# The softmax gate of two MoE dispatches: subtraction on VectorE and one exponential, or one exponential per tile with a bias on ScalarE

## The chip, the cores and the metric

The kernel runs on 1 core of one Trainium2 chip. The metric is the device time of one execution in microseconds (us). The core has five engines with in-order queues of their own: TensorE (PE in the profile; its weight loads are PEld), VectorE (DVE), ScalarE (ACT), GpSimd (POOL) and SyncE (SP). They meet at semaphores.

## What is computed

The input is 256 images of 128 channels by 7 x 7 places, 12,544 tokens in all. Six layers follow each other: a windowed attention, a 1x1-convolution attention, an attention without weights, a mixture of experts (192 hidden), an attention over three strides, and a second mixture of experts (512 hidden). The change touches the gates of the two mixtures, of which the reference says:

```python
scores = jnp.einsum('bne,ex->bnx', x, Wg) + bg
topk_vals, topk_idx = jax.lax.top_k(scores, TOP_K)      # 2 of 8 experts
gates = jax.nn.softmax(topk_vals, axis=-1)
```

(the second mixture takes the softmax of all eight first and normalises the two picked, which is the same pair of numbers). With the two largest logits a >= b of a token, the kernel makes ex = exp(b - a), den = 1 + ex, first gate = 1/den, second gate = 1 - first gate.

## The kernel before

The program is a chain of phases: windows, convolution, token dispatch "d2", experts "moe2", combine, scales with dispatch "d3", experts "moe3", final. All tensors of a layer pass through DRAM or the SBUF tensor X between phases. The trace has the dispatch d2 at about 575 to 872 us and the scales with d3 at about 1245 to 1808 us.

**What a dispatch does.** The class Dispatch (from L1186) works on chunks of tiles of 128 tokens: d2 has 24 chunks of 4 tiles and one of 2, d3 has 32 chunks of 3 and one of 2, 98 tiles each. For a chunk, TensorE turns X into token rows (`turn`), VectorE takes mean and variance (`stats`), ScalarE makes the inverse deviation (`rstd`, L1360 and L1362) and writes the normed rows (`norm`, L1371). VectorE scales the logits (`scale`, L1446), and `choose` takes the eight largest of each tile (L1457), subtracts the first from the second for the whole chunk (`gap`, L1465) and looks up the indices (L1467, two records a tile). `count_up` marks the picked experts (`pick`, L1477) and counts them, TensorE sums the counts into ranks (L1331 to L1336), `place` turns them into row numbers (L1503, L1510), and `weigh` takes the reciprocal of den (L1496). On ScalarE `gate` makes ex (L1380) and den (L1384), `names` writes token number and index (L1392, L1394), `second` the other gate (L1401). GpSimd then sends each tile's rows to their places with two indirect DMAs (`scatter`, L1558): 196 in each dispatch. ScalarE and either VectorE (d2) or GpSimd (d3) also split the next layer's expert weights in two (L1351 on ScalarE, L1421 behind it).

**What sets the order.** Every engine runs a list of calls written out by hand, one step per group of 8 images (32 groups). In d2 the gate of a chunk runs one step after its `choose`, ScalarE's step being rstd, expo, rstd, gate, turned, norm, v_out, names, second, split_high, square. In d3 one chunk goes through each step, and a step has four parts, p = 0 to 3. On VectorE p = 1 ends with `choose`, p = 2 begins with the residual (L1917) and the next score block (L1869, L1873) and ends with `count_up` and `weigh`, p = 3 has `factors` (L1911) and `place`. On ScalarE p = 2 is q_out (L2083), expo (L2103), `gate`, turned (L2132), inverses (L2122, L2124), square (L2049) and k_out (L2092); p = 3 ends with logvar (L2067), `names`, `second` and, in every third step, the weight split L1351. GpSimd's step is: adding the positions (L2013), four products of probabilities (L2004), L1985, L1973 and L1974, L1995, two scatters in each of three parts, and in every third step the weight split L1421, which waits for L1351. TensorE's last transposition before each score block (L1775) waits until VectorE has emptied the score bank (L1873), and ScalarE's L2132 waits for that transposition.

The semaphores that matter: `gate` waits for gap_done and for the last den; `choose` waits for gap_done of the chunk before ahead of L1457, and for ex_done of the chunk before ahead of L1465.

Of the kernel before, what the change touches and what calls it, by code (L numbers as in the profile page):

```python
# [19 lines left out]
ALU = mybir.AluOpType  # L20
ACT = mybir.ActivationFunctionType
AX_X = mybir.AxisListType.X

C = 128
# [60 lines left out]
class PhaseSemaphores:  # L85


    def __init__(self, nc, prefix):
        self.nc, self.prefix, self.held = nc, prefix, []
# [1096 lines left out]
class Dispatch:  # L1186
# [7 lines left out]
    def __init__(self, nc, sh, sb, sem, kind, e, wsplit, rows_dram, chunks, xt, small, joint=False):  # L1194

        self.joint, self.nc = joint, nc
        self.chunks, self.wide = chunks, max(n for _, n in chunks)
        self.quads = [(c, t0 + o, min(4, n - o), o) for c, (t0, n) in enumerate(chunks) for o in range(0, n, 4)]
        self.last_quad = [max(q for q, quad in enumerate(self.quads) if quad[0] == c) for c in range(len(chunks))]
        self.sh, self.e, self.wsplit, self.rows_dram, self.xt, self.small = sh, e, wsplit, rows_dram, xt, small  # L1200
        self.wg, self.bg = (sh.wg2, sh.bg2) if kind == "d2" else (sh.wg3, sh.bg3)
        self.w_in, self.bias_in = (sh.inputs["L2_ffn_W"], sh.inputs["L2_ffn_b"]) if kind == "d2" else (sh.inputs["L3_ffn_W"], sh.inputs["L3_ffn_b"])
        self.wgc = sb("wgc", [C, C + EXPERTS])
        self.below, self.ones, self.base16 = sb("below", [C, C], BF16), sb("ones", [C, C], BF16), sb("base16", [C, EXPERTS], BF16)
        self.below_f, self.ones_f = sb("below_f", [C, C]), sb("ones_f", [C, C])
        self.base8, self.tokens = sb("base8", [C, EXPERTS]), sb("tokens", [C, TILES])
        self.upto8, self.steps, self.blocks = sb("upto8", [C, EXPERTS * EXPERTS]), sb("steps", [C, STEPS]), sb("blocks", [C, NBLK])
        self.pad = sb("pad", [C, BLOCK // C, ROW])
        self.raw = [sb(f"raw{i}", [C, e.half]) for i in range(2)]
        self.wh, self.wl = [sb(f"wh{i}", [C, e.half], F32R) for i in range(2)], [sb(f"wl{i}", [C, e.half]) for i in range(2)]  # L1210
        self.st, self.mv = sb("dst", [C, QUAD, 6]), [sb(f"mv{i}", [C, QUAD, 2]) for i in range(2)]
        self.rs = [sb(f"drs{i}", [C, self.wide]) for i in range(2)]
        self.row = [sb(f"row{i}", [C, self.wide, ROW]) for i in range(self.NR)]
        self.lg = sb("lg", [C, self.wide, EXPERTS])
        self.top, self.idx = sb("top", [C, self.wide, 8]), [sb(f"idx{i}", [C, self.wide, 8], U32) for i in range(2)]
        self.pick = [sb(f"pick{i}", [C, self.wide, 2, EXPERTS]) for i in range(2)]
        self.seen = [sb(f"seen{i}", [C, 1 + self.wide, EXPERTS], BF16) for i in range(2)]
        self.gap, self.ex, self.den = sb("gap", [C, self.wide]), sb("ex", [C, self.wide]), sb("den", [C, self.wide])
        self.at = sb("at", [C, self.wide, 2, EXPERTS])
        self.pos = [sb(f"pos{i}", [C, self.wide, 2], U32) for i in range(self.NR)]  # L1220
        self.total, self.offs = sb("total", [C, EXPERTS]), sb("offs", [C, EXPERTS], I32)
        self.over, self.full = sb("over", [C, EXPERTS, STEPS]), sb("full", [C, EXPERTS])
        self.ends8, self.ends = sb("ends8", [C, EXPERTS, EXPERTS]), sb("ends", [C, EXPERTS])
        self.past, self.gone = sb("past", [C, NBLK, EXPERTS]), sb("gone", [C, NBLK, EXPERTS])
        self.begun, self.where = sb("begun", [C, NBLK]), sb("where", [C, NBLK])

        self.loaded, self.ready, self.centred = sem("loaded"), sem("ready"), sem("centred_gate")
        self.raw_loaded = [sem(f"raw_loaded{i}") for i in range(2)]
        self.high, self.low = sem("w_high"), sem("w_low")
        self.w_stored = [sem(f"w_stored{i}") for i in range(2)]  # L1230
        self.b_stored = sem("b_stored")
        self.xt_mm, self.log_mm, self.stat, self.mean_var = sem("turned"), sem("logits"), sem("stats"), sem("mean_var")
        self.ln_done, self.rs_done, self.normed = sem("logvar_d"), sem("rstd_d"), sem("normed_d")
        self.scaled, self.top_done, self.idx_done = sem("scaled"), sem("top"), sem("index")
        self.pick_done, self.seen_done = sem("picked"), sem("seen")
        self.count_done, self.pos_mm = sem("counted"), sem("pos_mm")
        self.gap_done, self.ex_done, self.den_done, self.g0_done = sem("gap"), sem("exped_d"), sem("den"), sem("g0")
        self.col_done, self.named = sem("columns"), sem("named")
        self.at_done, self.pos_done = sem("at"), sem("positions")
        self.scattered = [sem(f"scattered{i}") for i in range(self.NR)]  # L1240
        self.total_mm, self.tab, self.padded = sem("total_mm"), sem("table"), sem("padded")
# [132 lines left out]
    def gate(self, act, c):  # L1374
        nt = self.chunks[c][1]
        act.wait_ge(self.loaded, 16 * 8)
        act.wait_ge(self.gap_done, c + 1)
        if c >= 1:
            act.wait_ge(self.den_done, c)
        act.activation(self.ex[:, 0:nt], self.gap[:, 0:nt], ACT.Exp).then_inc(self.ex_done, 1)  # L1380
        act.wait_ge(self.ex_done, c + 1)
        if c >= 1:
            act.wait_ge(self.g0_done, c)
        act.activation(self.den[:, 0:nt], self.ex[:, 0:nt], ACT.Identity, bias=self.ones_f[:, 0:1]).then_inc(self.den_done, 1)  # L1384
# [65 lines left out]
    def choose(self, dve, c):  # L1450
        nt = self.chunks[c][1]
        lg, top, idx = self.lg, self.top, self.idx[c % 2]
        dve.wait_ge(self.scaled, c + 1)
        if c >= 1:
            dve.wait_ge(self.gap_done, c)
        for i in range(nt):
            last = dve.max(top[:, i, :], lg[:, i, :])  # L1457
        last.then_inc(self.top_done, 1)
        dve.wait_ge(self.top_done, c + 1)
        if c >= 1:  # L1460
            dve.wait_ge(self.ex_done, c)
        if c >= 2:
            dve.wait_ge(self.named, 2 * c - 2)
            dve.wait_ge(self.pick_done, c - 1)
        dve.tensor_tensor(self.gap[:, 0:nt], top[:, 0:nt, 1], top[:, 0:nt, 0], ALU.subtract).then_inc(self.gap_done, 1)  # L1465
        for i in range(nt):
            last = dve.max_index(idx[:, i, :], top[:, i, :], lg[:, i, :])  # L1467
        last.then_inc(self.idx_done, 1)
# [1458 lines left out]
```

## Time and profile before

| | us |
|---|---|
| three timed runs | 2283.72, 2289.64 (median), 2291.57 |
| profiled execution, whole | 2285.74 |
| profiled execution, span of the trace | 2284.1 |
| mean granted TensorE clock of the span | 0.891 of full |

The page shares the span as PE 78%, DVE 71%, ACT 61%, POOL 62% busy. Those are averages over eight phases with different limits, so for one phase only the rows of its own stretch count. The profiled execution's time is 1.6 us over its span and lies 3.9 us under the median of the timed runs.

### The profile page before, as it was taken

To read this page: it belongs to the slowest core of one execution; us is meant where nothing else is said; L and a number is where in the kernel's file an instruction comes from. 1 tells how busy PE (TensorE), PEld (TensorE's weight loads), DVE (VectorE), ACT (ScalarE), POOL (GpSimd) and SP (SyncE) were. 2 spreads that over 40 slices of the span, in tenths; PEclk is the share of its full clock that TensorE was granted. 3 is DMA by queue.
4 is the path that set the end of the run, shared out by engine and by line. 5 is a ranking of instruction groups with operands and counts; after the bars stand their busy time and mean duration, and the time that the engine had idled before them with its cause. 6 is when DMAs were issued, how large, how long until landed. Compare 5 with 4: busy or idle time off the path is not lost. (4 is left out here: it accounts for less than half of the span.)

```text
span 2284.1 us, 52612 instructions
## 1 busy us (share of the span) xinstructions
PE 1787.9 (78%) x16257; PEld 1236.1 (54%) x16257; DVE 1618.3 (71%) x4634; ACT 1404.3 (61%) x3208; POOL 1414.1 (62%) x1485
## 2 busy tenths in 40 slices
PE   7999997998777744777764777777786299999974
PEld 3555554776566643555543344444444177777763
DVE  5888887787677643666654588888786378888864
ACT  5777775564666523555540788888885267777750
POOL 3655554010177773777776378888888557767765
PEclk9999998999989857999985898998897599999995
DMA  6000000000221134666647012111110367777748
GB/s 116 17 0 0 0 0 2 1 0 18 74 83 55 55 89 124 185 180 179 174 122 249 9 60 68 55 56 55 60 36 30 98 222 232 227 231 234 226 131 338
DMA packets 169828, 233.57 MB, mean 102 GB/s; under 512 B 60032, under 2 KB 131957, under 8 KB 162190
## 3 DMA queue, kind: packets, MB, share of 16 engines
q1 hardware_dynamic: 142446, 172.32, 25.2%
q0 software_dynamic: 26880, 52.27, 6.8%
q10 hardware_dynamic: 288, 6.42, 0.7%
q8 instruction: 99, 1.62, 0.3%
q14 instruction: 115, 0.94, 0.1%
HBM read 155.37 MB, written 79.23 MB: 103 GB/s over the span
## 5 line engine op out<-in xcount | busy, mean ns | idle before, releaser
L2682 POOL DMA_INDIRECT expert_out<-moe_yr,moe_to x448 | 493.0, 1100 | 259.8 <-DVE moe_yr L2661 139.2
L1558 POOL DMA_INDIRECT expert_rows<-d_row,d_pos x392 | 380.8, 971 | 181.9 <-issue 164.8
L2597 ACT ACTIVATE moe_ah<-moe_hps,moe_w 128x512 f32<-128x512 f32 (+1 forms) x336 | 230.2, 685 | 204.3 <-PE moe_hps L2547 199.6
L2638 DVE TENSOR_TENSOR moe_hl<-moe_ah,moe_hh 128x512 fp32r<-128x512 f32 (+1 forms) x336 | 235.2, 700 | 95.6 <-ACT moe_hh L2602 89.3
L1775 PE MATMUL scales_ptps<-ident,scales_pr 113*128 113x113 f32 x512 | 104.2, 306 | 98.1 <-DVE scales_sc L1873 62.5
L550 POOL TENSOR_TENSOR window_pr<-window_pr,window_rc 113x392 f32<-113x392 f32 x128 | 108.9, 851 | 107.3 <-DVE window_rc L494 107.3
L2545 PE MATMUL moe_hps<-moe_xh,moe_w 128*128 128x512 f32 (+1 forms) x336 | 138.3, 412 | 35.5 <-DMA moe_w<-moe_split 31.4
L2533 PE MATMUL moe_xps<-ident,moe_xb 128*128 128x128 f32 x448 | 72.5, 286 | 102.6 <-DMA moe_xb<-expert_rows 102.6
L1775 PEld LDWEIGHTS scales_ptps<-ident,scales_pr 113*128 113x128 f32 x512 | 65.3, 157 | 152.3 <-DVE scales_sc L1873 68.7
L2557 PE MATMUL moe_yps<-moe_hh,moe_w 128*128 128x512 f32 (+1 forms) x336 | 144.3, 429 | 0.9 <-DVE moe_hl L2638 0.9
L538 POOL TENSOR_TENSOR window_sc<-window_sc,window_mx 113x392 f32<-113x392 f32 x128 | 107.8, 842 | 50.6 <-DVE window_mx L468 49.8
L2547 PE MATMUL moe_hps<-moe_xh,moe_w 128*128 128x512 f32 (+1 forms) x336 | 134.9, 401 | 0.0
L2546 PE MATMUL moe_hps<-moe_xl,moe_w 128*128 128x512 f32 (+1 forms) x336 | 134.5, 400 | 0.0
L2558 PE MATMUL moe_yps<-moe_hl,moe_w 128*128 128x512 f32 (+1 forms) x336 | 133.9, 398 | 0.0
L2559 PE MATMUL moe_yps<-moe_hh,moe_w 128*128 128x512 f32 (+1 forms) x336 | 133.3, 397 | 0.0
L2533 PEld LDWEIGHTS moe_xps<-ident,moe_xb 128*128 128x128 f32 x448 | 53.6, 144 | 134.2 <-DMA moe_xb<-expert_rows 125.3
L657 ACT ACTIVATE window_pt<-window_ptps 128x452 f32<-128x452 f32 x128 | 69.8, 545 | 90.9 <-PE window_ptps L334 90.8
L2004 POOL TENSOR_TENSOR scales_pr<-scales_pr,scales_fac 113x416 f32<-113x416 f32 x128 | 114.1, 903 | 2.7 <-DVE scales_fac L1911 1.3
L2627 DVE TENSOR_TENSOR moe_xl<-moe_xps,moe_xh 128x512 fp32r<-128x512 f32 x112 | 76.4, 682 | 54.6 <-ACT moe_xh L2590 54.6
L1071 POOL TENSOR_TENSOR conv_pr<-conv_pr,conv_rc 113x196 f32<-113x196 f32 x32 | 16.5, 516 | 154.4 <-DVE conv_rc L1037 154.4
L2602 ACT ACTIVATE moe_hh<-moe_ah 128x512 fp32r<-128x512 f32 (+1 forms) x168 | 106.2, 632 | 5.3
L2636 DVE CAST moe_hh<-moe_ah 128x512 fp32r<-128x512 f32 (+1 forms) x168 | 85.3, 508 | 27.1 <-ACT moe_ah L2597 27.1
(286 smaller groups left out, 5218.5 us busy)
## 6 DMA issues: line engine op xcount, KB each, us to landing
moe_w<-moe_split SPq DMA_DIRECT2D x56, 1026.5 KB
moe_xb<-expert_rows SPq DMA_DIRECT2D x112, 264.0 KB, 3.0
moe_w<-moe_split SPq DMA_DIRECT2D x56, 449.5 KB
c_yy<-expert_out SPq DMA_DIRECT2D x28, 448.0 KB, 7.1
final_yy<-expert_out SPq DMA_DIRECT2D x28, 448.0 KB, 7.7
expert_out<-moe_yr,moe_to POOLq DMA_INDIRECT x448
X<-in_x SPq DMA_DIRECT2D x32, 196.0 KB
expert_rows<-d_row,d_pos POOLq DMA_INDIRECT x392
```

What stands on the lines that cost most here:

```text
L1558: pool.indirect_dma_start(out=self.rows_dram, out_offset=bass.IndirectOffsetOnAxis(ap=self.pos[j][:, i, k:k + 1], axis=0), in_=self.row[j] ...
L1775: last = pe.transpose(ptps[:, hp * R:(hp + 1) * R], pr[at.r][p][:, 2 * hp:2 * hp + 2, :].rearrange("q h k -> q (h k)"), ident[0:R, 0:R])
L2533: last = pe.transpose(xps[:, t * C:(t + 1) * C], xb[b % NX][:, t, 0:C], ident[:, :])
L2545: pe.matmul(out, ww[:, W1H + k * P:W1H + (k + 1) * P], xh[j][:, :], start=True, stop=False)
L2546: pe.matmul(out, ww[:, W1H + k * P:W1H + (k + 1) * P], xl[j][:, :], start=False, stop=False)
L2547: pe.matmul(out, ww[:, W1L + k * P:W1L + (k + 1) * P], xh[j][:, :], start=False, stop=True).then_inc(h_mm, 1)
L2557: pe.matmul(out, ww[0:P, W2H + k * C:W2H + (k + 1) * C], high, start=(k == 0), stop=False)
L2558: pe.matmul(out, ww[0:P, W2H + k * C:W2H + (k + 1) * C], low, start=False, stop=False)
L2559: pe.matmul(out, ww[0:P, W2L + k * C:W2L + (k + 1) * C], high, start=False, stop=(k == K - 1)).then_inc(y_mm, 1)
L2597: act.activation(ah[n % NH][0:P, :], hps[n % 3][0:P, :], func, bias=bias(b, k)[0:P]).then_inc(h_done, 1)
L2638: dve.tensor_tensor(hl[n % NH][0:P, :], ah[n % NH][0:P, :], hh[n % NH][0:P, :].bitcast(F32), ALU.subtract).then_inc(hl_done, 1)
L2682: pool.indirect_dma_start(out=y_dram, out_offset=bass.IndirectOffsetOnAxis(ap=to[j][:, t:t + 1], axis=0), in_=yr[j][:, t, :], in_offset=No ...
```

## The change

The exponential of a chunk becomes one exponential for each of its tiles. Its input is the largest logit with scale -1, and its bias is the second largest, read from SBUF per partition. The subtraction, its tensor and its semaphore go. `gate` waits for top_done (the end of L1457) in place of gap_done; `choose` waits for ex_done of the chunk before ahead of L1457, where it waited for gap_done, and the later wait goes.

```diff
@@ Dispatch.gate
         act.wait_ge(self.loaded, 16 * 8)
-        act.wait_ge(self.gap_done, c + 1)
+        act.wait_ge(self.top_done, c + 1)
         if c >= 1:
             act.wait_ge(self.den_done, c)
-        act.activation(self.ex[:, 0:nt], self.gap[:, 0:nt], ACT.Exp).then_inc(self.ex_done, 1)
+        for i in range(nt):
+            last = act.activation(self.ex[:, i:i + 1], self.top[:, i, 0:1], ACT.Exp, scale=-1.0, bias=self.top[:, i, 1:2])
+        last.then_inc(self.ex_done, 1)
@@ Dispatch.choose
         if c >= 1:
-            dve.wait_ge(self.gap_done, c)
+            dve.wait_ge(self.ex_done, c)
         for i in range(nt):
             last = dve.max(top[:, i, :], lg[:, i, :])
         last.then_inc(self.top_done, 1)
         dve.wait_ge(self.top_done, c + 1)
-        if c >= 1:
-            dve.wait_ge(self.ex_done, c)
         if c >= 2:
             dve.wait_ge(self.named, 2 * c - 2)
             dve.wait_ge(self.pick_done, c - 1)
-        dve.tensor_tensor(self.gap[:, 0:nt], top[:, 0:nt, 1], top[:, 0:nt, 0], ALU.subtract).then_inc(self.gap_done, 1)
```

## Rows read from the trace of the kernel before

**Rows 1.** Busy time by stretch: length, PE, PEld, DVE, ACT, POOL, clock, DMA share, GB/s
```profile
575.00:872.00 297.00, 198.95 (x1623) 161.06 (x1621) 186.01 (x1009) 158.09 (x565) 188.73 (x196) 0.80 0.23 71
1335.00:1808.00 473.00, 345.27 (x4632) 213.84 (x4631) 372.76 (x1291) 360.33 (x915) 402.31 (x453) 0.86 0.17 55
```
**Rows 2.** GpSimd's groups, 620 to 868 us: busy, mean ns | idle before, releasers
```profile
L1558 POOL DMA_INDIRECT expert_rows<-d_row,d_pos x196 | 188.7, 963 | 121.3 <-issue 117.0 <-ACT d_row L1401 3.7 <-DVE d_pos L1510 0.3
```
**Rows 3.** GpSimd's waits, 1336 to 1808 us: total us, times, longest
```profile
POOL expert_rows L1558 <- issue: 47.8, 184, 1.4
POOL expert_rows L1558 <- ACT d_row L1401: 11.5, 6, 3.7
POOL d_wl L1421 <- ACT d_wh L1351: 6.7, 7, 1.9
POOL scales_wf L1995 <- ACT scales_rc L2124: 3.4, 3, 2.2
```
**Rows 4.** GpSimd's timeline in the steady steps of d3: start, length us
```profile
1513.61 0.99 POOL L1985 TENSOR_TENSOR scales_part<-scales_ef,scales_sm 113x384 f32<-113x384 f32 x1
...
1528.07 0.99 POOL L1985 TENSOR_TENSOR scales_part<-scales_ef,scales_sm 113x384 f32<-113x384 f32 x1
...
1531.52 0.90 POOL L2004 TENSOR_TENSOR scales_pr<-scales_pr,scales_fac 113x416 f32<-113x416 f32 x1
...
1533.01 0.86 POOL L1995 TENSOR_TENSOR scales_wf<-scales_ef,scales_rc 113x384 f32<-113x384 f32 x1
...
1554.44 2.38 POOL L1421 TENSOR_TENSOR d_wl<-d_raw,d_wh 128x1024 f32<-128x1024 f32 x1 [1.91 <-ACT d_wh L1351]
```
**Rows 5.** VectorE's groups by shape, 1300 to 1800 us: busy, mean ns | idle before
```profile
L1465 DVE TENSOR_TENSOR d_gap<-d_top 128x3 f32<-128x3 f32 x32 | 26.2, 819 | 1.1
```
**Rows 6.** VectorE's timeline: a step behind the weight split, then the next step
```profile
1512.39 2.25 DVE L1465 TENSOR_TENSOR d_gap<-d_top 128x3 f32<-128x3 f32 x1
1514.56 0.08 DVE L1467 MATCH_VALUE_LOAD d_idx<-d_top,d_lg 128x8 f32 x1
...
1528.60 0.49 DVE L1465 TENSOR_TENSOR d_gap<-d_top 128x3 f32<-128x3 f32 x1
1529.01 0.08 DVE L1467 MATCH_VALUE_LOAD d_idx<-d_top,d_lg 128x8 f32 x1
...
1532.03 0.47 DVE L1477 TENSOR_TENSOR d_pick<-iota,d_idx 128x48 f32<-128x48 f32 x1
```
**Rows 7.** ScalarE's timeline in the same steps
```profile
1522.78 0.29 ACT L1401 ACTIVATE d_row<-d_row,d_ones_f 128x3 f32<-128x3 f32 x1
1522.97 0.52 ACT L2074 ACTIVATE scales_rs<-scales_rs 128x392 f32<-128x392 f32 x1
...
1530.58 0.22 ACT L1380 ACTIVATE d_ex<-d_gap 128x3 f32<-128x3 f32 x1
1530.83 0.30 ACT L1384 ACTIVATE d_den<-d_ex,d_ones_f 128x3 f32<-128x3 f32 x1
1531.57 0.55 ACT L2132 ACTIVATE scales_pt<-scales_ptps 128x452 f32<-128x452 f32 x1 [0.44 <-PE scales_ptps L1775]
...
1532.31 0.28 ACT L2124 ACTIVATE scales_rc<-scales_rc 113x96 f32<-113x96 f32 x1
```
**Rows 8.** TensorE's timeline; L1708 in two steps
```profile
1535.58 0.93 PE L1708 MATMUL scales_vps<-scales_sq,mean_w 128*128 128x392 f32 x2
...
1545.67 0.32 PE L1775 MATMUL scales_ptps<-ident,scales_pr 113*128 113x113 f32 x1 [1.84 <-DVE scales_sc L1873]
...
1550.74 1.68 PE L1708 MATMUL scales_vps<-scales_sq,mean_w 128*128 128x392 f32 x2
```
**Rows 9.** L1465's busy time on VectorE in a stretch, then clock, DMA share, GB/s
```profile
1548.00:1556.00 8.00, 0.00 (x0) 0.63 0.06 19
```
**Rows 10.** Timeline at the first chunk of d2
```profile
608.58 0.17 DVE L1465 TENSOR_TENSOR d_gap<-d_top 128x4 f32<-128x4 f32 x1
608.66 0.08 DVE L1467 MATCH_VALUE_LOAD d_idx<-d_top,d_lg 128x8 f32 x1
...
614.61 0.19 ACT L1380 ACTIVATE d_ex<-d_gap 128x4 f32<-128x4 f32 x1
...
617.51 0.32 ACT L1401 ACTIVATE d_row<-d_row,d_ones_f 128x4 f32<-128x4 f32 x1
...
618.86 1.14 POOL L1558 DMA_INDIRECT expert_rows<-d_row,d_pos  x1 [61.79 <-issue]
```

More of the change, by code:

```diff
@@ L1217, in __init__ @@
         self.seen = [sb(f"seen{i}", [C, 1 + self.wide, EXPERTS], BF16) for i in range(2)]
-        self.gap, self.ex, self.den = sb("gap", [C, self.wide]), sb("ex", [C, self.wide]), sb("den", [C, self.wide])
+        self.ex, self.den = sb("ex", [C, self.wide]), sb("den", [C, self.wide])
         self.at = sb("at", [C, self.wide, 2, EXPERTS])
@@ L1236, in __init__ @@
         self.count_done, self.pos_mm = sem("counted"), sem("pos_mm")
-        self.gap_done, self.ex_done, self.den_done, self.g0_done = sem("gap"), sem("exped_d"), sem("den"), sem("g0")
+        self.ex_done, self.den_done, self.g0_done = sem("exped_d"), sem("den"), sem("g0")
         self.col_done, self.named = sem("columns"), sem("named")
```

## Prediction, made before the changed kernel ran

> **What bounds the kernel now.** Only the two dispatches are touched, so I read their stretches and not the page's averages. First the busy time by stretch. In d2 no engine is busy throughout: GpSimd's 188.73 of 297 us is the scatters alone. In 1335 to 1808 us, where the scales phase sorts, GpSimd leads with 402 of 473 us, before DVE with 373 and ACT with 360 [rows 1]. Then what ends the idle time of that engine. In d2 its 196 scatters take 0.963 us each and are followed by about 0.3 us of issue; 188.7 + 117.0 us of issue (61.8 of which is the idle stretch before the first one) is 244, the whole time from the first scatter to the last. It waited for ScalarE in no way that one sees: 3.7 us in the same 0.3 us pieces [rows 2]. So d2 ends when GpSimd has issued its list, and the only thing that can move it is the start of the list.
>
> In d3 GpSimd's busy time and its 47.8 us of issue make 450 of 473 us. What is left is nearly all ScalarE's doing: 11.5 us in 6 waits for L1401, 6.7 us in 7 for the weight split L1351, 3.4 us in 3 for L2124, 21.6 us in 16 waits [rows 3]. Between them GpSimd is packed; a step without a weight split lasts 14.45 us on it (L1985 at 1513.61 and 1528.07 lie one step apart [rows 4]). **So time in d3 can only be won or lost at those 16 waits, or by a step that becomes longer than GpSimd's own.**
>
> **The row that surprises.** The subtraction of 128x3 numbers takes 819 ns on average in d3, 26.2 us for 32 [rows 5], where the same work with 4 columns takes 0.17 us in d2 [rows 10]. The timeline tells why. In one step it lasts from 1512.39 to 1514.64, and GpSimd's L1985 ends at 1514.60; in the next it lasts from 1528.60 to 1529.09, and L1985 ends at 1529.06 [rows 4, 6]. It ends 0.03 to 0.04 us behind a GpSimd product both times: it waits for GpSimd. The Trainium skill has the reason, SBUF — State Buffer, "Who interferes with whom": a VectorE instruction with two SBUF inputs and a GpSimd instruction that reads SBUF take one shared port in turn, each for its whole length. By that rule, the trace agrees.
>
> **The change part by part.** *VectorE, removed.* In d2 start to start the subtraction costs 608.66 - 608.58 = 0.08 us [rows 10]. In d3 it is 1529.01 - 1528.60 = 0.41 us in an ordinary step, and 1514.56 - 1512.39 = 2.17 us in the step behind a weight split, where GpSimd is late [rows 6].
> *Who gets it.* What follows on VectorE is the index search, with no stall in these rows, the residual and the score block, whose L1873 frees TensorE's last transposition, for which TensorE waited 1.84 us [rows 8] and ScalarE's L2132 0.44 us [rows 7]. So up to here the 0.41 us is real. Then comes L1477, also a two-input instruction: it runs 1532.03 to 1532.50, ending 0.08 us behind GpSimd's L2004 of 1531.52 to 1532.42. Begun 0.41 us earlier it begins at 1531.62, still inside L2004, and ends when it ends now [rows 4, 6]. So the part of the step behind L1477 gets nothing from an ordinary step, and up to 0.41 us where L1477 slips in ahead of L2004.
> *ScalarE, added.* 196 exponentials replace 58, all with a bias read from SBUF. No row shows an exponential with such a bias on one column. The nearest is L1401, 3 columns with bias and scale: 0.29 us long, but the next instruction starts 0.19 us behind it [rows 7]. The bounds per further start are 0.10 (the 0.29 us less 0.19 of overlap, a start that costs only its remainder) and 0.29 us (no overlap at all). I take 0.19, being the measured spacing of that form. The last one is 0.29 long where the old one was 0.19 to 0.22. With 3 tiles: 2 x 0.19 + 0.10 = +0.48 us; with 4 tiles 3 x 0.19 + 0.10 = +0.67 us. Bounds with 3 tiles 0.3 to 0.7 us.
> By the Trainium skill, ScalarE: Activation LUTs, "Rules for kernel authors", the budget is about 0.3 us for each activation with a bias pointer; taken as serial work, an estimate from it is 3 x 0.3 - 0.22 = +0.68 us a step, and d3 would then be the slower rival below.
> *What hides it in d3.* The gate ended at 1531.13 and L2132 began at 1531.57, behind a wait of 0.44 us that ends on VectorE's path [rows 7]. VectorE's path comes 0.41 us earlier, ScalarE's 0.48 us later: L2132 starts at 1531.61, +0.04 us. L2124 ends at 1532.59 + 0.04, GpSimd wants it at 1533.01 [rows 4]: 0.38 us to spare. If this cover were gone, each step would cost 0.48 us, 15.4 us for 32.
> *The 13 waits for L1401 and L1351.* These stand behind TensorE: in the step of the weight split GpSimd waited 1.91 us for L1351 [rows 4], the granted clock was 0.63 in that stretch [rows 9], which is a time partly at the lower level, and L1708, which ScalarE needs, took 1.68 in place of 0.93 us [rows 8]. TensorE began this run at 1545.67, released by L1873 [rows 8], which comes 0.41 us earlier without the subtraction. So each wait shrinks by between 0 (L1477 holds the later score block where it is) and 0.41 us. I take 0.3, nearer the upper end, since L1873 lies ahead of L1477: 13 x 0.3 = **-3.9 us**. The bounds are 0 and -5.3. The three waits for L2124 lie in the tail, behind 1727 us, where the subtraction no longer stalls; I take 0 for them, at most 3 x 0.48 = +1.4.
> *Steps behind a weight split* give VectorE 2.17 us, but GpSimd is packed there; 0 us, unless the lead survives to the next wait (a rival).
> *d2.* ScalarE runs without a gap from L1380 at 614.61 to L1401 at 617.51, and the first scatter follows that [rows 10]: +0.67 - 0.08 = **+0.6 us** at the start of a packed list. Bounds 0.2 and 1.0. The other 24 gates are hidden by the list.
> *Waits moved.* ex_done of the chunk before, now ahead of L1457: in d2 `weigh`, earlier in VectorE's step, has already waited for den, which comes behind ex; in d3 the gate is a step old. 0 us. Behind `weigh`'s wait for den in d3 the gate has over 1 us to spare.
> *Sum:* -3.9 + 0.6 = -3.3 us. Against the profiled execution, 2285.74 - 3.3 = 2282.4; the median of the runs lies 3.9 above it, so 2286.3.
>
> **The rivals.** *1, the lead is kept (faster).* The 2.17 us and the 0.41 us carry VectorE and ScalarE ahead through L1477 and on to the weight split; TensorE idles less and keeps its upper clock. GpSimd then never waits for L1351 or L1401. Of 6.7 + 11.5 us [rows 3] the first wait, 3.7 us, stays, as it is the filling of the pipeline: -14.5 + 0.6 = -13.9 us, 2275.7. For it: TensorE's wait of 1.84 us is VectorE's, and the 1.91 us depends on a clock that was down. Against it: TensorE's transpositions also need GpSimd's products, which come no sooner.
> *2, ScalarE becomes the one waited for (slower).* At the 16 places where GpSimd waits for ScalarE already, the gate stands in the same queue ahead of all three instructions. If ScalarE's waits for TensorE shrink away there, as VectorE's path gets shorter, each grows by 0.48 us: 16 x 0.48 = +7.7, with d2 +8.3 us, 2297.9. It decides as soon as a gate costs more than ScalarE waits behind it, 0.44 us in an ordinary step. At the upper bound of 0.7 us it would be 16 x 0.7 + 1.0 = +12. Against it: ScalarE's idle time in a step is several such waits, and L1351 is late through TensorE.
> *3, the stall only moves.* The change removes the subtraction but not the wait for GpSimd's port: L1477 or the next two-input instruction pays it, and nothing before it was late. d3 0, d2 +0.6: 2290.2, no change.
>
> **How the numbers follow.** About 0.3% (6.9 us) is what a measurement of this kernel tells from no change. The forecast has 0.45, its own range -6 to +3 and so "same"; rival 1 0.25, rival 2 0.15, rival 3 0.15. A tenth of rival 1 and of the others ends inside 0.3% too, as a partial effect. Faster 0.25, same 0.61, slower 0.14. The range for 8 in 10: below to rival 1's value less the spread of the runs, 2274; above, to the forecast's bounds and rival 3 with the runs' own spread of some 4 us, 2294, which leaves most of rival 2 out.
>
> **What would show it.** Right: L1380 with 196 records near 0.29 us, starting about 0.19 apart; GpSimd's list in d2 still without gaps and 0.6 us later; in d3 L2132's wait for TensorE close to 0, GpSimd's waits for L1351 shorter by about 0.3 each, and L1477 longer than its 0.47 us now. Wrong: those waits gone (rival 1) or each longer (rival 2), single activations spaced by 0.29 us, or a change of more than 7 us in the stretch 1335 to 1808 us; any change in the length of a phase other than the two dispatches would be no effect of this edit.

## The result, and the profile after

The changed kernel takes 2304.89 us in the median of four runs (2299.97 to 2308.60), the kernel before 2289.21 in four runs beside it (2283.72 to 2291.57). The ratio is 1.0074, 95% interval [1.0050, 1.0098]: it is slower, and 2304.89 lies above my range, which ended at 2294. I had forecast 2286.3 us and no change. The profiled execution took 2304.61 us with a span of 2302.8, 18.7 us above the span of before. In the experiments below, one run of one kernel (the marks reduced, 2721.34 us at a granted clock of 0.57) was in a slow state and is left out of its ratio.

In the changed kernel the lines behind the edit are renumbered: L1457 is L1459, L1467 is L1466, L1477 is L1476, L1482 is L1481, L1401 is L1403, L1558 is L1557, L1873 is L1872, L1775 is L1774, L1995 is L1994, L2004 is L2003, L2124 is L2123, L1421 is L1423 and L1351 keeps its number. L1465 is gone, and the exponentials are L1381.

First the stretches that hold the two dispatches, from the first scatter's surroundings on; the columns are those of [rows 1], to which these answer:

```profile
575.00:884.00 309.00, 205.67 (x1620) 166.45 (x1618) 184.81 (x984) 174.69 (x638) 188.74 (x196) 0.78 0.22 68
1346.50:1825.30 478.80, 345.25 (x4628) 218.97 (x4620) 360.40 (x1259) 369.76 (x977) 401.70 (x452) 0.85 0.16 53
```

GpSimd's busy time has not moved (188.73 and 188.74; 402 and 402 us). All loss is idle time of GpSimd. From the first to the last scatter d2 went from 247.2 to 255.6 us and d3 from 470.5 to 478.8 us, 16.7 us together. The experts' phase behind d2, which the edit does not touch, was 6.5 us longer in this profile (329.2 against 322.7 us). Over the twelve kernels below it lies anywhere between 321.9 and 327.7 us whatever was done to d2, and the changed kernel's is 1.5 us beyond that; I give it no cause. The pieces between the phases give back 4.5 us.

GpSimd's group in d2 and its waits in d3, which answer to [rows 2] and [rows 3]:

```profile
L1557 POOL DMA_INDIRECT expert_rows<-d_row,d_pos x196 | 188.7, 963 | 128.7 <-issue 119.7 <-ACT d_row L1403 8.7 <-DMA expert_rows<-d_row,d_pos 0.3
```

```profile
POOL scales_wf L1994 <- ACT scales_rc L2123: 15.3, 12, 2.6
POOL expert_rows L1557 <- ACT d_row L1403: 7.1, 4, 2.2
POOL d_wl L1423 <- ACT d_wh L1351: 6.0, 4, 2.3
```

The three kinds of wait were 21.6 us in 16 pieces and are 28.4 us in 20. The waits for L1401 and L1351, on which I had put my gain, went from 18.2 to 13.1 us (5.1, where 3.9 was forecast). But 3.7 us of the first and 2.2 us of the second are the wait ahead of the first scatter; from the first to the last scatter it is 14.5 and 10.9 us. And the wait for L2124, which I had priced at 0, went from 3.4 to 15.3 us.

How far one profile can be trusted in d3 is told by the kernels below that have the same d3. The three with the d3 of before (before, d2 alone, before with d2's gate earlier) last 470.5, 476.6 and 473.3 us there, the three with the changed d3 (changed, d3 alone, changed with d2's gate earlier) 478.8, 481.2 and 476.2. The waits for L1401 and L1351 are 14.5, 20.3 and 17.4 us against 10.9, 18.4 and 10.7: shorter by 4 us on average, but with overlap. The waits for L2124 are 3.4, 3.6 and 3.3 against 15.3, 10.6 and 13.5, and leave no doubt. So a difference of less than about 6 us in the length of d3 says nothing by itself.

The exponentials themselves are as forecast, on average 288 ns (ScalarE's group by shape, whole kernel), and four of them take 0.83 us with the next instruction at 0.87, so a further one starts 0.18 to 0.19 us behind the last (ScalarE's timeline in d2):

```profile
L1381 ACT ACTIVATE d_ex<-d_top 128x1 f32<-128x1 f32 x196 | 42.3, 288 | 0.0
```

```profile
646.63 0.83 ACT L1381 ACTIVATE d_ex<-d_top 128x1 f32<-128x1 f32 x4
647.50 0.30 ACT L1386 ACTIVATE d_den<-d_ex,d_ones_f 128x4 f32<-128x4 f32 x1
```

### The profile page after: what moved, and what is told of

It reads as the page before. It is cut to its first block and busy times, and to the rows that moved or that the text cites. A ratio compares the mean times of both kernels' runs of the same rounds, so it can differ in the third digit from the quotient of the medians.

```text
span 2302.8 us, 52636 instructions
## 1 busy us (share of the span) xinstructions
PE 1793.9 (78%) x16257; PEld 1245.8 (54%) x16257; DVE 1605.7 (70%) x4576; ACT 1430.9 (62%) x3346; POOL 1416.0 (61%) x1485
## 5 line engine op out<-in xcount | busy, mean ns | idle before, releaser
L1557 POOL DMA_INDIRECT expert_rows<-d_row,d_pos x392 | 380.9, 972 | 184.6 <-issue 167.6
L1774 PE MATMUL scales_ptps<-ident,scales_pr 113*128 113x113 f32 x512 | 100.1, 304 | 104.1 <-POOL scales_pr L2003 51.2
L1774 PEld LDWEIGHTS scales_ptps<-ident,scales_pr 113*128 113x128 f32 x512 | 63.8, 157 | 153.9 <-POOL scales_pr L2003 71.7
L2003 POOL TENSOR_TENSOR scales_pr<-scales_pr,scales_fac 113x416 f32<-113x416 f32 x128 | 114.1, 903 | 2.6 <-DVE scales_fac L1910 1.1
```

Of the source, the lines that this page charges most:

```text
L1557: pool.indirect_dma_start(out=self.rows_dram, out_offset=bass.IndirectOffsetOnAxis(ap=self.pos[j][:, i, k:k + 1], axis=0), in_=self.row[j] ...
L1774: last = pe.transpose(ptps[:, hp * R:(hp + 1) * R], pr[at.r][p][:, 2 * hp:2 * hp + 2, :].rearrange("q h k -> q (h k)"), ident[0:R, 0:R])
```

## The experiments

Two parts of the change (ScalarE's gate and VectorE's subtraction) act in two places (d2 and d3). The first four kernels take them apart, the next four test what undoes the loss, the last four test whether the explanation adds up.

### d2 alone, d3 alone

Every Dispatch gets a flag. Where it is not set, the subtraction, its waits and the single exponential of before stay.

```diff
+        self.apart = kind == "d2"        # "d3" in the second kernel
...
-        act.wait_ge(self.top_done, c + 1)
+        act.wait_ge(self.top_done if self.apart else self.gap_done, c + 1)
```

> The change in the first dispatch (d2) alone; d3 keeps subtraction and one exponential. Theory A (in d2 GpSimd's list had almost no backlog, so 0.67 us more of ScalarE in each of 25 gates lets it run dry): d2, from its first to its last scatter, is longer by about 8 us than before (255.6 against 247.2 us), with waits of GpSimd for L1403 of about 8 us; the whole kernel +7 us by d2, and by up to 6.5 more if moe2 is slower only because of how d2 leaves it. Rival B (the time is lost in d3, d2's loss in the one profile is chance): whole kernel within 3 us of before.

> The change in the second dispatch (d3) alone; d2 is as before. Theory A (each dispatch loses by itself): the stretch from the first to the last scatter of d3 about 8 us longer than before's 470.5, the stretch before it about 3 shorter, the kernel +5 us; moe2 as before, 322.6 us. Rival B (d3 loses only because the phases before it leave it shifted): d3 as before, the kernel within 2 us.

Measured: d2 alone 1.0034 [1.0005, 1.0063], d3 alone 1.0025 [1.0003, 1.0047]. In the profiles d2 alone lengthens d2 to 251.3 us (I had expected 255.6), d3 alone lengthens d3 to 481.2 us and leaves d2 at 246.9. Both places cost, 8.2 and 6.0 us in the medians, together 14.3 of the 15.7 us of the whole change, which is as near as the intervals allow. So neither of my two sub-forecasts (+0.6 in d2, -3.9 in d3) holds.

### ScalarE's part alone, VectorE's part alone

The first keeps the subtraction and makes one exponential for each tile, with a column of zeros as its bias. The second drops the subtraction and takes one exponential of the largest logit alone; the second largest is left out of the gate, so its gate is not the softmax any more.

```diff
-        act.activation(self.ex[:, 0:nt], self.gap[:, 0:nt], ACT.Exp).then_inc(self.ex_done, 1)
+        for i in range(nt):
+            last = act.activation(self.ex[:, i:i + 1], self.gap[:, i:i + 1], ACT.Exp, bias=self.below_f[:, 0:1])
+        last.then_inc(self.ex_done, 1)
```

```diff
-        for i in range(nt):
-            last = act.activation(self.ex[:, i:i + 1], self.top[:, i, 0:1], ACT.Exp, scale=-1.0, bias=self.top[:, i, 1:2])
+        last = act.activation(self.ex[:, 0:nt], self.top[:, 0:nt, 0], ACT.Exp, scale=-1.0)
```

> ScalarE's part alone: an exponential for each tile with a bias pointer (a column of zeros), its input the subtraction's result, which stays on VectorE. The output is the reference's. Theory A (ScalarE's queue is what costs): as slow as the changed kernel or a few us slower, 2300 to 2310, with VectorE's subtraction still stalled in d3. Rival B (the loss comes from VectorE's order and the moved wait): near before, 2290.

> VectorE's part alone: the subtraction is gone and ScalarE makes one exponential for the chunk, of minus the largest logit (the second largest is left out of the gate, so that the output is not the reference's). Theory A (the port stall on VectorE cost time): d3 shorter by 3 to 15 us, d2 the same, the kernel 2275 to 2287. Rival B (the stall was not on the path, or moves to the next instruction with two SBUF inputs): within 3 us of before, with the pick's (L1477 of before) mean above its 469 ns in d3.

Measured: ScalarE's part 1.0058 [1.0036, 1.0080], VectorE's part 1.0057 [1.0032, 1.0081]. Each costs nearly as much as both together, so they do not add. For VectorE's part this is against both things that I had expected, a gain or no change. By stretches: ScalarE's part makes d2 254.1 us and d3 475.8, VectorE's part leaves d2 at 247.8 and makes d3 499.2. So **d2's loss is ScalarE's alone**, and **taking the subtraction away is in itself a loss in d3**, a large one as long as the gate stays short. The 475.8 us of ScalarE's part in d3 lie inside the 470.5 to 476.6 us of the kernels with the d3 of before, so a loss by the gate alone is not shown there. GpSimd's waits in d3 for VectorE's part alone:

```profile
POOL expert_rows L1556 <- ACT d_row L1402: 25.3, 10, 2.8
POOL d_wl L1422 <- ACT d_wh L1351: 20.8, 7, 3.0
```

The waits that my forecast wanted to shrink have grown from 18.2 to 46.1 us (14.5 to 43.8 without the one ahead of the first scatter).

### What d2 loses: GpSimd's start

GpSimd's timeline of d2 in the changed kernel has six gaps over the usual 0.30 us of issue; in the kernel before it has none after the first scatter:

```profile
651.36 0.96 POOL L1557 DMA_INDIRECT expert_rows<-d_row,d_pos  x1 [2.86 <-ACT d_row L1403]
684.48 0.96 POOL L1557 DMA_INDIRECT expert_rows<-d_row,d_pos  x1 [3.14 <-ACT d_row L1403]
715.86 0.96 POOL L1557 DMA_INDIRECT expert_rows<-d_row,d_pos  x1 [1.20 <-ACT d_row L1403]
726.62 0.96 POOL L1557 DMA_INDIRECT expert_rows<-d_row,d_pos  x1 [0.94 <-ACT d_row L1403]
757.51 0.96 POOL L1557 DMA_INDIRECT expert_rows<-d_row,d_pos  x1 [0.78 <-issue]
769.84 0.97 POOL L1557 DMA_INDIRECT expert_rows<-d_row,d_pos  x1 [1.27 <-issue]
```

They add up to 10.19 us, less 6 x 0.30 that would be there anyhow is 8.4 us: the whole growth of d2, 255.6 - 247.2. In the ten kernels of the study whose gate is short or runs earlier, no scatter behind the first one waits. The list had been packed without being far ahead of starving. Counted on GpSimd's timeline, the 25th scatter is the first of the fourth chunk; it started at 649.55 in the kernel before, and ScalarE's L1401 for it had ended at 646.07. A scatter that waits starts 0.87 us behind that instruction (651.36 less 650.49 in the changed kernel), so there were 649.55 - 646.07 - 0.87 = 2.6 us in hand. The edit took more (L1401 of the fourth chunk, before and after):

```profile
645.75 0.32 ACT L1401 ACTIVATE d_row<-d_row,d_ones_f 128x4 f32<-128x4 f32 x1
```

```profile
650.17 0.32 ACT L1403 ACTIVATE d_row<-d_row,d_ones_f 128x4 f32<-128x4 f32 x1
```

That is 4.4 us later, though the first one had come 1.1 us earlier (616.40 against 617.51): 5.5 us lost between the first and the fourth chunk. Only three gates run in between, and each is 0.64 us longer, 1.9 us in all. The rest is TensorE. These are the windows between the two instructions, before and after (columns of [rows 1]):

```profile
617.51:645.75 28.24, 21.56 (x204) 17.16 (x203) 23.70 (x126) 20.83 (x76) 20.49 (x21) 1.00 0.43 140
```

```profile
616.40:650.17 33.77, 26.12 (x203) 20.29 (x203) 23.73 (x122) 22.85 (x84) 23.75 (x24) 0.85 0.38 125
```

The same number of matmuls takes 26.12 in place of 21.56 us, because the granted clock is 0.85 and no longer 1.00, that is, partly the lower level. The gate stands on ScalarE just ahead of L2413 (now L2412), which empties the bank that TensorE needs for its L2288 (now L2287), and TensorE's idle time in front of that is longer by 0.64 us, the gate's own growth. These are its four matmuls behind the first gate, before and after:

```profile
615.90 0.63 PE L2288 MATMUL d_turn<-ident,d_xn 128*128 128x128 f32 x4 [1.49 <-issue]
```

```profile
614.77 0.91 PE L2287 MATMUL d_turn<-ident,d_xn 128*128 128x128 f32 x4 [2.13 <-issue]
```

Right behind this first longer wait the same four matmuls take 0.91 in place of 0.63 us, so the clock has fallen already (in the three other kernels with the longer wait L2287 first takes longer than 0.63 us, 0.88 to 1.09, two turns later). The clock goes with the wait in all fourteen kernels of the study. In the four whose d2 gate is long and in its old place (the change, d2 alone, ScalarE's part, the marks reduced) the waits behind the first two gates are 2.13 or 2.14 us, and the clock of the stretch 617 to 650 us is 0.84 to 0.89. In the ten others these waits are 1.06 to 1.07 us (gate moved, next section) or 1.48 to 1.49 us, and the clock is 1.00.

### The gate one step of the list earlier

If d2's loss is where the gate stands in ScalarE's list, moving it into a wait heals it. In d2 the gate is called at the end of the step before, behind the squares, where ScalarE waits for VectorE's statistics anyway (0.94 to 1.44 us in front of L1360 up to 650 us, in the kernel before).

```diff
-                for c in chunks(s - 2):
-                    d.gate(act, c)
...
                 if group(s + 4):
                     square(s + 4)
+                for c in chunks(s - 1):
+                    d.gate(act, c)
```

> The kernel before, with d2's gate one step earlier on ScalarE, behind square at the end of its step, where ScalarE is about to wait about 1.3 us for the variances. Theory A (d2's GpSimd list has almost no backlog): no gain for d2's end, since the list is packed in the kernel before: d2 247 us, the kernel within 2 us of before. If d2 gets shorter than 246 us, the list was not what bounds it.

> The changed kernel with the same move of d2's gate. Theory A (0.67 us more in ScalarE's part of the step that TensorE and VectorE wait for is what made GpSimd's list run dry in d2): d2 goes back from 255.6 to about 247 to 249 us and the kernel gains about 7 us, to 2298. Rival (d2's loss comes from elsewhere, such as the moved wait): no gain.

Measured: on the kernel before 1.0002 [0.9986, 1.0018], on the changed kernel 1.0003 [0.9981, 1.0025]. The changed kernel is back at the time of before, and its d2 lasts 246.7 us with the clock at 1.00 in the first chunks. The kernel before gains nothing, d2 246.6 us: there the list was packed already. The changed kernel was not timed again in this round, so its gain is read against the kernel before. The explanation of d2 holds: its 8.4 us hang on where 0.64 us of ScalarE stand in its list.

### The marks without a second input

In d3 GpSimd's port stall was to vanish with the subtraction, or to move to the picks (my third rival). VectorE's groups by shape in d3 (busy us, mean ns | idle before), before and then after:

```profile
L1465 DVE TENSOR_TENSOR d_gap<-d_top 128x3 f32<-128x3 f32 x31 | 25.6, 826 | 1.1
L1477 DVE TENSOR_TENSOR d_pick<-iota,d_idx 128x48 f32<-128x48 f32 x31 | 14.8, 478 | 0.0
L1482 DVE TENSOR_TENSOR d_seen<-d_pick 128x24 bf16<-128x24 f32 x31 | 8.8, 283 | 1.1
```

```profile
L1476 DVE TENSOR_TENSOR d_pick<-iota,d_idx 128x48 f32<-128x48 f32 x31 | 21.5, 694 | 0.0
L1481 DVE TENSOR_TENSOR d_seen<-d_pick 128x24 bf16<-128x24 f32 x31 | 12.0, 388 | 1.1
```

The three took 49.2 us and the two that are left take 33.5. The means hide two kinds of marks: 27 of the 31 last 0.18 to 0.31 us, as all of them do in the kernel before, and four last up to 1.39 us. VectorE lost 25.6 us of work and got 9.9 us of longer ones, in a worse place: behind the score block that frees TensorE, but ahead of the next one and of the ranks. To test it, the changed kernel gets its marks as a reduction over one input, which does the same sum:

```diff
-        dve.tensor_tensor(seen[:, 1:1 + nt, :], pick[:, 0:nt, 0, :], pick[:, 0:nt, 1, :], ALU.add).then_inc(self.seen_done, 1)
+        dve.tensor_reduce(seen[:, 1:1 + nt, :], pick[:, 0:nt, :, :].rearrange("p t k e -> p t e k"), AX_X, ALU.add).then_inc(self.seen_done, 1)
```

(in d3; d2 keeps the old form), and a second kernel is the one before with this and with the subtraction as one instruction for each tile, whose second operand is a number per partition:

```diff
-        dve.tensor_tensor(self.gap[:, 0:nt], top[:, 0:nt, 1], top[:, 0:nt, 0], ALU.subtract).then_inc(self.gap_done, 1)
+        for i in range(nt):
+            last = dve.tensor_scalar(self.gap[:, i:i + 1], top[:, i, 1:2], top[:, i, 0:1], None, ALU.subtract)
+        last.then_inc(self.gap_done, 1)
```

> The changed kernel, and in d3 the counts of picked experts (seen) come from a reduction over the two picks, which has one SBUF input, in place of an addition with two. The output is the reference's. Theory C (the wait for GpSimd's port is not won by dropping the subtraction: it moves behind the score block to the pick and to seen, ahead of TensorE's ranks, and costs there): VectorE's stalls in d3 fall by what seen had over its free 0.19 us, and the kernel gains 2 to 6 us on the changed one, that is 2299 to 2303 against 2305; the pick keeps its 0.7 us. Rival D (only ScalarE's longer queue costs, the port plays no part): as the changed kernel within 2 us.

> The kernel before, with two of d3's three two-input VectorE instructions of the gate rebuilt with one SBUF input: the subtraction as one instruction a tile with the largest logit as a per-partition operand, seen as a reduction. ScalarE's work is the old one. The output is the reference's. Theory C: the wait goes to the pick alone, which becomes longer than its 0.47 us; if stalls behind the score block are what costs, the kernel is as before or slower by up to 8 us; with the wait gone for good it would be 2 to 10 us faster. Rival D: within 2 us of before.

Measured: the changed kernel with the reduction 1.0000 [0.9981, 1.0018], d3 469.6 us; the kernel before with both forms 0.9932 [0.9909, 0.9955], d3 468.0 us. The reduction takes 204 ns on average, 208 at most, and never waits. Three subtractions by a number per partition take 207 ns each, 0.46 us together, and never wait. The picks did not take the wait over as I expected (482 ns against 478). The kernel with both forms is faster than the one before and the changed one.

The changed kernel with reduced marks has a d2 still 254.8 us long, and yet its time is that of before. Its ratio is 0.7% under the changed kernel's, about 16 us, where d3 is only 9.2 us shorter. With intervals of 0.2% to either side of both ratios most of the rest may be noise; it is not explained.

### Both cures together, each form alone, and the faster one again

> The changed kernel with both cures at once: in d2 the gate is called one step earlier on ScalarE, behind the squares, and in d3 the marks (seen) are one reduction of one input. If d2's loss is ScalarE's longer gate ahead of the row writes and d3's loss is the port stall that moves on to the marks, the two add: each alone gave back 8 to 9 of the 15.7 us, so this lies 0 to 4 us under before, with d2 near 247 us and d3 near 470 us from first to last scatter. Rival, both cures act on one and the same wait further down: no better than one of them, that is the time of before within 3 us, with one stretch still about 8 us longer than in before. Rival, ScalarE's added 0.48 us a step in d3 is itself a loss: d3 stays some 5 us over before's.

> The kernel before, with only the subtraction of d3 as one instruction per tile with the largest logit as its per-partition operand (in place of one instruction with two SBUF inputs). If the port is taken by instructions with two tensor inputs alone, the three take about 0.6 us together and never wait for GpSimd; the stall moves to the next one with two inputs, so pick and seen grow as in the changed kernel (pick 0.69, seen 0.39 us mean): time of before to 8 us slower. Rival, the stall vanishes and nothing takes its place: d3 shorter by 5 us or more, 0.3 to 0.7 per cent faster.

> The kernel before, with only the marks (seen) of d3 as one reduction of one input. If what counts is the last instruction with two inputs ahead of TensorE's ranks, this alone gains some of what both forms together gained (15.6 us): 3 to 8 us faster, seen 0.20 us mean, subtraction and pick as in before. Rival, the subtraction's form is what gained: time of before within 3 us, since seen waits only 8.8 us in all in the kernel before.

> The kernel before, with both forms in d3: the subtraction as one instruction per tile with a per-partition operand, the marks as one reduction. The same kernel as the earlier one whose time was 0.9932 of before. If the gain is the port's, it comes again, 0.991 to 0.996, with d3 some 3 to 8 us shorter than in before; if that was a chance of few runs, it lies within 0.3 per cent.

Measured: both cures 0.9985 [0.9967, 1.0003], d2 246.8 and d3 469.9 us; the form of the subtraction alone 1.0091 [1.0068, 1.0114], d3 497.8 us; the form of the marks alone 0.9991 [0.9974, 1.0007], d3 474.2 us; both forms again 0.9968 [0.9950, 0.9986], d3 467.5 us. In the stretches the cures add: both d2 and d3 are as short as in the kernel before, where each cure alone left one of them long (254.8 and 476.2 us). In the ratios it is not shown, since each alone gave 1.0000 and 1.0003 already and the intervals overlap. The gain of both forms is real, 6 us in the medians here and 11 us the first time. The marks' form alone gains nothing that stands clear of the noise, where I had expected 3 to 8 us.

The subtraction's form alone is the clearest kernel of the study: the gate on ScalarE is the old one, VectorE has the same result at the same place, only the stall of L1465 is gone, and the kernel is 21 us slower, where I had expected 8 at most. The semaphores that the change moves stand here as before, so they have no part in this loss. Its marks now take the stall, in 17 of 33 chunks for about 1.38 us each and in one for 0.88:

```profile
L1487 DVE TENSOR_TENSOR d_seen<-d_pick 128x24 bf16<-128x24 f32 x31 | 27.0, 869 | 1.1
L1482 DVE TENSOR_TENSOR d_pick<-iota,d_idx 128x48 f32<-128x48 f32 x31 | 15.5, 500 | 0.0
L1467 DVE TENSOR_SCALAR d_gap<-d_top 128x1 f32<-128x1 f32 x95 | 14.4, 207 | 1.3 <-DVE d_top L1457 0.2
```

One step of it, from VectorE to GpSimd (here L1878 empties the score bank, L1780 is the transposition, L1713 the variance, L2072 what ScalarE makes of it):

```profile
1563.11 1.38 DVE L1487 TENSOR_TENSOR d_seen<-d_pick 128x24 bf16<-128x24 f32 x1
1565.33 0.59 DVE L1878 TENSOR_TENSOR scales_sc<-scales_sps,scales_mx 113x416 f32<-113x416 f32 x1
1565.97 0.45 PE L1780 MATMUL scales_ptps<-ident,scales_pr 113*128 113x113 f32 x1 [0.77 <-DVE scales_sc L1878]
1567.94 1.67 PE L1713 MATMUL scales_vps<-scales_sq,mean_w 128*128 128x392 f32 x2
1569.64 0.59 ACT L2072 ACTIVATE scales_rs<-scales_vps,eps 128x392 f32<-128x392 f32 x1 [1.50 <-PE scales_vps L1713]
1570.51 1.05 ACT L1351 ACTIVATE d_wh<-d_raw 128x1024 fp32r<-128x1024 f32 x1
1571.63 2.37 POOL L1421 TENSOR_TENSOR d_wl<-d_raw,d_wh 128x1024 f32<-128x1024 f32 x1 [2.98 <-ACT d_wh L1351]
```

The marks last until 1564.49, 0.05 us behind the end of GpSimd's L2000, the L1995 of before (1563.58 to 1564.44). The next score block is late, TensorE runs its variance in 1.67 us where 0.93 is its time at the full clock, ScalarE waits 1.50 us for that, and GpSimd 2.98 for the weight split; the clock of 1563 to 1571 us is 0.60. In the faster kernel (both forms, second time) the same step has no long marks, L1717 (the variance) takes 0.93 us, the clock is 1.00 and GpSimd waits 0.35 us. Its timeline and the clock of the 8 us around it:

```profile
1540.79 0.21 DVE L1489 TENSOR_REDUCE d_seen<-d_pick 128x24 bf16<-128x48 f32 x1
1543.75 0.93 PE L1717 MATMUL scales_vps<-scales_sq,mean_w 128*128 128x392 f32 x2
1546.70 2.38 POOL L1421 TENSOR_TENSOR d_wl<-d_raw,d_wh 128x1024 f32<-128x1024 f32 x1 [0.35 <-ACT d_wh L1351]
```

```profile
1541.00:1549.00 8.00, 6.10 (x108) 4.14 (x104) 6.23 (x19) 7.23 (x16) 7.15 (x8) 1.00 0.06 19
```

From the marks' start to the variance's end it is 6.50 us here and 3.89 there, 2.61 more, and GpSimd waits 2.63 us more. Of the 2.61 the marks are 1.17 (1.38 less 0.21); the other 1.44 go with TensorE's lower clock, 0.74 of them in the variance itself. TensorE's wait for the score bank is not longer (0.77 us, 1.02 in the faster kernel), so the delay comes through VectorE's end and the clock. What lowered the clock is not shown: TensorE's matmuls were slow before these marks began (L1704 at 1562.44 took 1.52 us for two, 0.93 in the faster kernel).

By the Trainium skill, SBUF — State Buffer, "Who interferes with whom", VectorE contends with GpSimd only with two SBUF inputs, and then against an instruction that reads SBUF, or in a mode that uses both port pairs, and a reduction never does on this chip. The traces agree: the marks as a reduction take 204 ns on average in each of the five kernels that have it, while the marks as an addition with two inputs range from 283 to 869 ns for the same work.

## All of d3 in one table

GpSimd's waits are nearly all that differ. Lengths from first to last scatter of the profiled executions, waits of GpSimd for ScalarE and VectorE in that stretch (without the one ahead of the first scatter, 2.2 to 3.7 us), mean time of the three instructions in question:

| kernel | d3, us | waits, us | subtraction, picks, marks, ns |
|---|---|---|---|
| before | 470.5 | 18.8 | 826, 478, 283 |
| changed | 478.8 | 26.8 | none, 694, 388 |
| VectorE's part | 499.2 | 48.6 | none, 730, 848 |
| subtraction by a number per partition | 497.8 | 47.0 | 3 x 207, 500, 869 |
| changed, both cures | 469.9 | 17.7 | none, 740, 204 |
| both forms, second time | 467.5 | 15.5 | 3 x 207, 479, 204 |

Length less waits is 450.6 to 452.2 us in all six. Picks that wait (740 ns) cost little. Marks that wait in every second chunk (17 and 18 of 33) cost 20 us and more, and the reduction in their place takes d3 from 497.8 back to 467.5 us.

**What ScalarE's longer gate does in d3.** GpSimd waits for L2124 (now L2123) in 12 places of the changed kernel. In this one ScalarE runs from the gate on without a gap, and L1994 comes 0.92 us late:

```profile
1595.24 0.67 ACT L1381 ACTIVATE d_ex<-d_top 128x1 f32<-128x1 f32 x3
1595.95 0.30 ACT L1386 ACTIVATE d_den<-d_ex,d_ones_f 128x3 f32<-128x3 f32 x1
1596.15 0.53 ACT L2131 ACTIVATE scales_pt<-scales_ptps 128x452 f32<-128x452 f32 x1
1597.24 0.87 POOL L1994 TENSOR_TENSOR scales_wf<-scales_ef,scales_rc 113x384 f32<-113x384 f32 x1 [0.92 <-ACT scales_rc L2123]
```

The same place in the faster kernel, whose gate is short:

```profile
1571.60 0.22 ACT L1380 ACTIVATE d_ex<-d_gap 128x3 f32<-128x3 f32 x1
1571.85 0.30 ACT L1384 ACTIVATE d_den<-d_ex,d_ones_f 128x3 f32<-128x3 f32 x1
1572.05 0.53 ACT L2141 ACTIVATE scales_pt<-scales_ptps 128x452 f32<-128x452 f32 x1
1573.14 0.87 POOL L2004 TENSOR_TENSOR scales_wf<-scales_ef,scales_rc 113x384 f32<-113x384 f32 x1 [0.44 <-ACT scales_rc L2133]
```

The gate and what follows it take 1596.15 - 1595.24 = 0.91 us against 1572.05 - 1571.60 = 0.45, and the wait is 0.92 against 0.44. The added 0.46 us arrives at GpSimd in full here. There are 12 such waits in each kernel; 8 of them measure 0.86 to 0.92 us in the changed one, 7 of them 0.34 to 0.47 in the faster one. But the totals do not give the gate's price. The two kernels with reduced marks and a long gate have 10.1 and 12.2 us of waits for L2124, the two with reduced marks and a short gate 11.9 and 10.2. All of GpSimd's waits in d3 are 18.1 and 17.7 us in the first two and 15.6 and 15.5 in the others, so with the marks out of the way the longer gate costs about 2 us there.

## Why the prediction was wrong

**d2, +0.6, with "the other 24 gates are hidden by the list".** This step failed: 8.4 us. I read a packed list as a list far behind its suppliers. Its fourth chunk had 2.6 us in hand and the edit took 4.4, as ScalarE's +0.64 a gate lengthened TensorE's idle time and the clock fell from 1.00 to 0.85 there. I had seen how long a gate became and priced only its first occurrence. The start of the list was not the only thing that could move its end.

**ScalarE's size, +0.48 and +0.67.** Right: 0.46 us a step of three (0.91 less 0.45), 0.64 a step of four, spacing 0.18 to 0.19.

**What hides it in d3, L2132's wait of 0.44 and 0.38 us to spare at L2124, and "I take 0 for L2124".** Failed. The cover was read in a step where VectorE's path was late. Where ScalarE has no wait ahead of L2132 nothing hides the gate: the wait for L2124 grew by 11.9 us where I had put 0. What share is the gate's length stays open. The faster kernels have 10.2 and 11.9 us of this wait with a short gate, but VectorE's part and the subtraction's form alone have only 4.0 and 3.0 with the stall of L1465 gone just the same, and ScalarE's part alone 5.5. It grows where neither L1465 nor, in most steps, the marks stall.

**d3, 13 waits x -0.3.** The size was about right (18.2 to 13.1 us in the changed kernel; 3.6 us between the scatters, and 4 on average of three profiles each), but the reason was not, so this is luck. With the subtraction gone and the gate short, the same waits grew to 46.1 us, since the marks took over the stall. In the changed kernel the two edits partly undo each other: its marks stall in 4 chunks and not in 17, and take 388 ns on average and not 848. That this is because ScalarE, and L1994 with it, come later is argued and not shown.

**"L1477 takes part of it back."** Right as far as it goes (picks 478 to 694 ns). But I stopped at the first instruction with two inputs behind the gap; the second, the marks, stands directly ahead of a score block and is the costly one.

**The rivals.** Rival 2 had the right side and nearly the right place: ScalarE becomes the one waited for, 2297.9. It was too small, as it priced d2 at its first gate and left out the marks. Rival 3 had the right mechanism, the stall moves, and a wrong price, 0. Rival 1 did not come with this edit, whose waits for L1351 and L1401 are still 13.1 us. With both forms changed they are 6.3 and 7.9 us, 3.6 of it ahead of the first scatter, and that kernel is faster, by 11 and 6 us.

**What stays open.** Why the marks meet GpSimd's L1995 in 18 of 33 chunks of one kernel (869 ns on average) and in none of the one before (283) is a matter of some tenths of a microsecond that I can't forecast. That the lower clock in d2's first chunks follows from TensorE's longer waits is argued from fourteen kernels that agree, and not from one that changed TensorE's idle time alone. And the time that the reduced marks give back in the changed kernel is more than its d3 shows.

## What to carry to other kernels

An engine that issues without gaps may still be only a few microseconds ahead of starving: compare, at its first chunks, when the last input was ready and when it was taken, before calling anything upstream hidden. A stall at a shared port need not go with the instruction that shows it; here it moved to a later instruction of the same kind, and what counted was who waits behind that one. Make all of them of a kind that did not wait here (a reduction at 204 ns, an operand per partition at 207), or leave the stall where it hurts least: here one stall in the right place was worth 21 us.

## What was not expected of the hardware

A subtraction with a number per partition as its operand never waited for GpSimd: 95 of them at 207 ns, where the same with two tensors took 826 ns for three columns. And the changed kernel's picks lasted from 1562.36 to 1563.88 us once, although GpSimd was in a scatter until 1562.88 and began its product only at 1562.90:

```profile
1562.36 1.52 DVE L1476 TENSOR_TENSOR d_pick<-iota,d_idx 128x48 f32<-128x48 f32 x1
```

```profile
1561.92 0.96 POOL L1557 DMA_INDIRECT expert_rows<-d_row,d_pos  x1 [0.30 <-issue]
1562.90 0.91 POOL L2003 TENSOR_TENSOR scales_pr<-scales_pr,scales_fac 113x416 f32<-113x416 f32 x1
```

So an instruction that comes to the port during a scatter can stay behind the next product as well; in d2, where GpSimd does nothing but scatters, the subtractions of four columns took 166 ns on average in the kernel before. Which of the two it was here, the end of the scatter or the start of the product, was not tried.
